# Convolution spans 12 to 15 of group 1 one a tile in tiles 2 to 5, with tile 0 reordered, span 31 moved to ScalarE and GpSimd, and the last sums in a free buffer

## The chip, the core and the metric

The kernel runs on one core of a Trainium2 chip. The metric is the device time of one execution in microseconds (us). Engines are named as the profile names them: PE (TensorE), DVE (VectorE), ACT (ScalarE), POOL (GpSimd), and SP, whose queue starts nearly all transfers.

## The reference

`x` is (128, 32, 512): 128 samples n, 32 channels c, 512 positions. Every (sample, channel) pair is one token of 512 values.

```python
y   = conv1d(x, weight, groups=4, kernel 9, padding 4) + cond @ c_weight.T + bias   # a shift per (n, c)
yq  = fake_quant(y,  per token)                  # scale = max|y| / 127, round, clip
h   = silu(yq @ wq_gate.T) * (yq @ wq_up.T)      # 512 -> 1376, weights fake-quantized per row
out = x + fake_quant(h, per token) @ wq_down.T   # 1376 -> 512
```

`fake_quant` rounds to whole steps of a scale that is the largest absolute value over 127, so a token can't be quantized before all of it is known.

## The kernel before

The 32 channels are 32 **tiles** of 128 tokens. Each tile goes through the same steps:

- PE multiplies the tile's quantized tokens by the gate and by the up weights, each in three **pieces** of 512, 512 and 352 columns (4 matmuls a piece, line 1043). Gate pieces go to PSUM banks 0 and 1, up pieces to 2 and 3, in turn, so a piece waits until the piece two before it in the same kind has been read out.
- DVE scales a gate piece (`scale_gate`, line 793), ACT takes SiLU (line 628), POOL multiplies by the weights' scales (`scale_silu`, line 517), and DVE multiplies by the up piece (`multiply_up`, line 803). Its last piece done, DVE takes the tile's largest value (`token_scales`, line 809), and ACT rounds (`round_h`, line 633) and converts (`convert_h`, line 641). SP's queue transposes the result.
- PE multiplies tile i - 4 by the down weights (`down`, 11 matmuls, line 1063), DVE scales it (line 821), POOL adds the residual (line 525), SP stores it.

The input of the tiles is made beside this. The convolution is done in four **groups** of 8 channels, and each group in eight **spans** of 64 positions, numbered 0 to 31: spans 8 to 15 are group 1, 24 to 31 group 3. A span is 5 float32 matmuls on PE (`conv_span`, line 927). Its result leaves PSUM in one of two ways: DVE adds the shift while it copies (`add_shift`, line 723), or, for the spans of the list `BY_ACT`, ACT copies (line 566) and POOL adds the shift later (`shift_span`, line 492). DVE folds two spans into running maxima (`fold_y`, line 735). After a group's last fold it makes the scale and the inverse, ACT rounds the group's channels (`round_y`, line 573), POOL converts them (line 482) and SP transposes them. Group 1 is needed from tile 8 on, group 3 from tile 24 on.

Tables set where this stands: `SPANS_AT` (the tile whose `for` body holds a span's matmuls and its reading), `SHIFTS_AT` (POOL's shifts), `FOLDS_AT` and `EARLY_FOLDS_AT` (DVE's folds), `CHANNELS_AT` (rounding and conversion). Every engine runs its own instructions strictly in the written order. In one tile PE's order is gate piece 0, gate 1, up 0, `down` of tile i - 4, the spans, gate 2, up 1, up 2; in tile 4 alone `down(0)` stands between up 1 and up 2. DVE's order in tile i is `scale_gate` 0, `multiply_up(i - 1, 2)`, `scale_gate` 1, `token_scales(i - 1)`, `multiply_up` 0, the down scaling, `scale_gate` 2, `add_shift`, `multiply_up` 1, the folds, and in tiles 0 to 2 the maxima of a quarter of the down weights (`weights_down`, line 711).

The first tiles also finish the weights: the last gate and up rows (`round_w(10)`, `turn_gate_up(10)`, `copy_gate_up(10)`), the rows of scales (`turn_xq`, `copy_xq`), and the down weights (`weights_down` on DVE, `round_down` on ACT line 578, `convert_down` on POOL line 473), one quarter a tile.

Of the kernel before, what the change touches and what calls it, by code (L numbers as in the profile page):

```python
# [27 lines left out]
def adaln_ffn(nc, x, x_windows, cond_ctx_bias, taps_cut, w_gate_up, w_down, out):  # L28
# [39 lines left out]
    with ExitStack() as ctx:  # L68
# [98 lines left out]

        BY_ACT = [2, 3, 4, 5] + list(range(SPANS, 2 * SPANS + 2))
        BY_DVE = [q for q in range(SLOTS) if q not in BY_ACT]
# [90 lines left out]

        SPANS_AT = {0: [9, 10], 1: [11], 2: [12, 13], 3: [14, 15]}
        SPANS_AT.update({5 + i: [16 + i] for i in range(SPANS)})
        SPANS_AT.update({17 + i: [24 + 2 * i, 25 + 2 * i] for i in range(SPANS // 2)})
# [13 lines left out]

        SHIFTS_AT = {1: [8, 9], 2: [10, 11], 3: [12, 13], 4: [14, 15], 5: [16], 6: [17]}
        EARLY_FOLDS_AT = {6: [15]}
        FOLDS_AT = {3: [9], 4: [11], 5: [13]}  # L280
        FOLDS_AT.update({i: [q for q in at if q % 2] for i, at in SPANS_AT.items() if at[0] >= 2 * SPANS + 2 and at[-1] % 2})
        FOLDS_AT[7] = [2 * SPANS + 1]

        def down_bank_of(i):
# [14 lines left out]
        def _(sp):  # L299
# [56 lines left out]
            def store(i):  # L356
                sp.wait_ge(out_ready, i + 1)
                sp.dma_start(out[:, i, :], xo_of(i))\
                    .then_inc(stored[i % XO_BUFS] if i < TILES - LATE else late_stored, 16)

            def store_last(half):
                cols = slice(HALF * half, HALF * (half + 1))
                sp.wait_ge(out_ready, TILES + half)
                sp.dma_start(out[:, TILES - 1, cols], xo_of(TILES - 1)[:, cols]).then_inc(late_stored, 16)
# [79 lines left out]
        def _(pool):  # L444
# [82 lines left out]
            for i in range(TILES):  # L527
                scale_silu(i, 0)
                if i == 0:
                    round_w(JT - 1)  # L530
                if i >= LAG + 1:
                    add_residual(i - LAG - 1)
                scale_silu(i, 1)
                if i == 0:

                    pool.wait_ge(w_turned, JT)
                    for b in range(HQ_BUFS):
                        pool.memset(hq[b][:, INTER:JT * P], 0.0).then_inc(pad_zero, 1)
                for o in down_at(i - 1):
                    convert_down(o)  # L540
                for n in EARLY_CHANNELS_AT.get(i, []):
                    convert_y(n)
                scale_silu(i, 2)
                for n in CHANNELS_AT.get(i, []):
                    convert_y(n)
                for q in SHIFTS_AT.get(i, []):
                    shift_span(q)
# [4 lines left out]
        def _(act):  # L552
# [92 lines left out]
            copy_xq(4)  # L645
            copy_span(8)
            silu(0, 1)
            copy_gate_up(8)
            copy_gate_up(9)
            copy_gate_up(10)  # L650
            copy_xq(5)
            copy_xq(6)
            for i in range(TILES):
# [3 lines left out]
                if i == DOWN_ROW_AT + 1:  # L657
                    copy_down_row()
                for o in down_at(i - 1):
                    round_down(o)  # L660
# [19 lines left out]
        def _(dve):  # L680
# [151 lines left out]
            for i in range(TILES):  # L832
# [12 lines left out]
                else:  # L845
                    for o in down_at(-1):
                        weights_down(o)
                folds(EARLY_FOLDS_AT.get(i, []))
                multiply_up(i, 0)
                if i == 0:  # L850
                    multiply_up(i, 1)
                    for o in down_at(0):
                        weights_down(o)
                if LAG < i < TILES - 1:
# [29 lines left out]
            def finish_last_but_one():  # L884
                i = TILES - 2
                dve.wait_ge(late_residuals_in, 16)

                dve.wait_ge(out_ready, i)
                dve.wait_ge(down_scaled, i + 1)
                dve.tensor_tensor(xo_of(i), xo_of(i), down_out[:, i % 2, :], ALU.add).then_inc(out_ready, 1)  # L890

            finish_last_but_one()

            def finish_last(half):
                i = TILES - 1
                cols = slice(HALF * half, HALF * (half + 1))
                part = down_out[:, i % 2, cols]
                if half == 0:

                    dve.wait_ge(out_ready, i - 1)  # L900
                dve.wait_ge(last_down_done, half + 1)
                dve.scalar_tensor_tensor(part, gate_bank[half][:, 0:HALF], h_scale[:, i:i + 1],
                                         wd_scale_row[:, cols], ALU.mult, ALU.mult).then_inc(last_down_scaled, 1)
                if half == 0:

                    dve.wait_ge(out_ready, i)
                dve.wait_ge(last_down_scaled, half + 1)
                dve.tensor_tensor(xo_of(i)[:, cols], xo_of(i)[:, cols], part, ALU.add).then_inc(out_ready, 1)

# [4 lines left out]
        def _(pe):  # L914
# [153 lines left out]
            for i in range(TILES):  # L1068
# [10 lines left out]
                if i == 0:  # L1079
# [5 lines left out]
                    turn_xq(5)  # L1085
                    turn_xq(6)
                if LAG < i < TILES - 1:
# [80 lines left out]
```

## Time and profile before

| | |
|---|---|
| median of 3 runs | 294.94 us (294.86 to 295.38) |
| the profiled execution | 295.01 us, of which its span is 293.4 us |
| granted TensorE clock | 1.00 |
| PE busy | 282.5 us, 96% of the span |
| DVE, ACT, POOL busy | 251.5, 194.1, 200.8 us |

The span runs from the first to the last instruction; 1.6 us of the execution lie around it. "Busy" of PE includes the pipelined ends of matmuls, so short waits between matmuls don't show as idle time on the page and are read from the chain of waits or from the weight loads.

### The profile page before, as it was taken

The numbers are of one execution on the slowest core, as the hardware profiler recorded it, in microseconds if no ns is written. First come the engines' busy times: TensorE is split into PE (matmuls) and PEld (weight loads), VectorE is DVE, ScalarE is ACT, GpSimd is POOL, SyncE is SP. The second block draws the span as 40 slices with busy tenths as digits, with TensorE's granted clock in tenths as the row PEclk, the third lists the DMA queues.
The fourth block names the chain that finished last, engine by engine and source line by source line (L and its number), as shares of the span: only waits on it lengthen the run. The fifth ranks groups of instructions, "written<-read, shape, count | busy, mean of one in ns | idle before, by whom it ended". The sixth has DMA issues, their size and how long they took to land.

```text
span 293.4 us, 4778 instructions
## 1 busy us (share of the span) xinstructions
PE 282.5 (96%) x1621; PEld 164.4 (56%) x1621; DVE 251.5 (86%) x406; ACT 194.1 (66%) x231; POOL 200.8 (68%) x212
## 2 busy tenths in 40 slices
PE   7998889999999999999999999999999999999994
PEld 7887656654555555555444566655444444444443
DVE  3879789999999997988988878898988889888885
ACT  2259889997777666654778845354788866666640
POOL 1595959998777667653788846552778887666623
PEclk9999999999999999999999999999999999999999
DMA  7999943479967867755389997526355683433345
GB/s 264 413 408 358 412 112 59 106 168 292 208 154 167 189 153 172 204 150 146 102 214 304 221 270 199 156 59 93 104 156 156 159 194 96 87 86 90 101 98 196
DMA packets 83847, 53.36 MB, mean 182 GB/s; under 512 B 69904, under 2 KB 70672, under 8 KB 83696
## 3 DMA queue, kind: packets, MB, share of 16 engines
q1 hardware_dynamic: 83536, 52.89, 67.3%
q10 hardware_dynamic: 288, 0.18, 0.3%
q8 instruction: 13, 0.21, 0.3%
q14 instruction: 10, 0.08, 0.1%
HBM read 27.75 MB, written 8.39 MB: 123 GB/s over the span
## 4 chain that ended last, share of the span: by engine, by line
PE 76%; DVE 11%; DMA 4%; POOL 3%; issue 2%; SPq 2%; ACT 1%; POOLq 1%; DVEq 0%
PE bank L1043 45%; PE bank L1063 21%; PE bank L927 9%; DMA slab<-x_windows 4%; DVE h_max L809 2%; DVE h_mem L803 2%; DVE gu_max L694 2%; DVE y_part L735 1%; SPq L308 1%; SPq L316 1%; POOL h_mem L465 1%; DVE sg_mem L793 1%; DVE y_mem L723 1%; POOL sg_mem L517 1%; POOLq L68 1%
## 5 line engine op out<-in xcount | busy, mean ns | idle before, releaser
L1043 PE MATMUL bank<-wgu_t,xq_mem 128*128 128x512 bf16 (+1 forms) x768 | 155.9, 357 | 1.5 <-DVE h_mem L803 1.0
L517 POOL TENSOR_TENSOR sg_mem<-sg_mem,gu_scale_row 128x512 f32<-128x512 f32 (+1 forms) x96 | 111.3, 1162 | 65.5 <-ACT sg_mem L628 65.5
L1043 PEld LDWEIGHTS bank<-wgu_t,xq_mem 128*128 128x128 bf16 x768 | 73.8, 98 | 73.6 <-DVE h_mem L803 8.4
L628 ACT ACTIVATE sg_mem<-sg_mem,x_scale 128x512 f32<-128x512 f32 (+1 forms) x96 | 63.6, 674 | 44.1 <-DVE sg_mem L793 43.7
L1063 PE MATMUL bank<-wd_t,hq_mem 128*128 128x512 bf16 (+1 forms) x341 | 78.6, 379 | 0.0
L803 DVE SCALAR_TENSOR_TENSOR h_mem<-bank,x_scale,sg_mem 128x512 f32<-128x512 f32 (+1 forms) x96 | 66.4, 692 | 11.8 <-POOL sg_mem L517 10.7
L793 DVE TENSOR_TENSOR sg_mem<-bank,gu_scale_row 128x512 f32<-128x512 f32 (+1 forms) x96 | 60.2, 628 | 14.3 <-PE bank L1043 14.1
L633 ACT ACTIVATE h_mem<-h_mem,h_inv 128x1376 f32<-128x1376 f32 (+1 forms) x32 | 45.3, 1415 | 28.7 <-DVE h_inv L687 28.6
L1063 PEld LDWEIGHTS bank<-wd_t,hq_mem 128*128 128x128 bf16 (+1 forms) x341 | 33.3, 98 | 40.4 <-DMA hq_mem<-hq_mem 0.5
L809 DVE TENSOR_REDUCE h_max<-h_mem 128x1 f32<-128x1376 f32 x32 | 50.5, 1577 | 0.0
L927 PE MATMUL bank<-toeplitz_cut,slab 128*128 128x160 f32 (+1 forms) x320 | 44.8, 291 | 2.4 <-DMA slab<-x_windows 1.8
L927 PEld LDWEIGHTS bank<-toeplitz_cut,slab 128*128 128x128 f32 x320 | 43.6, 191 | 5.6 <-DMA slab<-x_windows 2.6
L641 ACT ACTIVATE hq_mem<-h_mem 128x1376 bf16<-128x1376 f32 (+1 forms) x32 | 41.9, 1309 | 0.1
L525 POOL TENSOR_TENSOR xo_mem<-xo_mem,hq_mem 128x512 f32<-128x512 f32 x24 | 30.5, 1270 | 0.0
L821 DVE SCALAR_TENSOR_TENSOR hq_mem<-bank,h_scale,wd_scale_row 128x512 f32<-128x512 f32 x31 | 23.0, 743 | 1.3 <-POOL slab L525 1.3
L573 ACT ACTIVATE y_mem<-y_mem,x_inv 128x512 f32<-128x512 f32 x24 | 16.0, 707 | 0.3 <-DVE x_inv L687 0.3
L735 DVE TENSOR_REDUCE y_part<-y_mem 128x8 f32<-128x1024 f32 x12 | 14.6, 1215 | 1.7 <-POOL y_mem L492 1.6
L465 POOL TENSOR_SCALAR hq_mem<-hq_mem,gu_inv 128x512 f32<-128x512 f32 (+1 forms) x14 | 9.4, 692 | 6.5 <-DVE gu_inv L707 6.2
L482 POOL TENSOR_SCALAR yq_mem<-y_mem 128x512 bf16<-128x512 f32 x22 | 13.3, 620 | 0.2 <-ACT y_mem L573 0.2
L585 ACT ACTIVATE wgu_t<-bank 128x1024 bf16<-128x1024 int16 (+1 forms) x11 | 10.6, 1004 | 3.7 <-PE bank L943 3.6
L694 DVE TENSOR_REDUCE gu_max<-hq_mem 128x2 f32<-128x1024 f32 (+1 forms) x7 | 8.5, 1211 | 5.2 <-DMA hq_mem<-w_gate_up 5.2
L723 DVE TENSOR_TENSOR y_mem<-bank,shift 128x512 f32<-128x512 f32 x18 | 11.9, 681 | 0.7 <-PE bank L927 0.7
(63 smaller groups left out, 136.4 us busy)
## 6 DMA issues: line engine op xcount, KB each, us to landing
slab<-x_windows SPq DMA_DIRECT2D x32, 320.0 KB, 5.0
xo_mem<-x SPq DMA_DIRECT2D x24, 256.0 KB, 3.0
out<-xo_mem SPq DMA_DIRECT2D x24, 256.0 KB, 2.2
hq_mem<-w_gate_up SPq DMA_DIRECT2D x6, 512.0 KB, 6.7
slab<-w_down SPq DMA_DIRECT2D x3, 688.0 KB, 12.5
h_mem<-w_gate_up SPq DMA_DIRECT2D x4, 512.0 KB, 14.1
slab<-x SPq DMA_DIRECT2D x1, 2048.0 KB, 9.1
out<-slab SPq DMA_DIRECT2D x7, 256.0 KB, 2.0
```

What stands on the lines that cost most here:

```text
L517: pool.tensor_tensor(s, s, gu_scale_row[:, 1, at:at + n], ALU.mult).then_inc(silu_scaled, 1)
L525: pool.tensor_tensor(xo_of(i), xo_of(i), down_out[:, i % 2, :], ALU.add).then_inc(out_ready, 1)
L628: act.activation(s, s, ACT.Silu, scale=x_scale[:, i:i + 1]).then_inc(silu_done, 1)
L633: act.activation(hi, hi, ACT.Copy, bias=MAGIC, scale=h_inv[:, i:i + 1]).then_inc(h_rounded, 1)
L641: act.activation(hq[i % HQ_BUFS][:, first:INTER], h[i % H_BUFS][:, first:], ACT.Copy, bias=-MAGIC)\
L793: dve.tensor_tensor(sg[i % SG_BUFS][:, at:at + n], gate_bank[(NP * i + p) % 2][:, 0:n], gu_scale_row[:, 0, at:at + n], ALU.mult).then_inc( ...
L803: dve.scalar_tensor_tensor(h[i % H_BUFS][:, at:at + n], up_bank[(NP * i + p) % 2][:, 0:n], x_scale[:, i:i + 1], sg[i % SG_BUFS][:, at:at + ...
L809: dve.tensor_reduce(h_max[:, one], h[i % H_BUFS], AX_X, ALU.max, apply_absolute_value=True)\
L821: dve.scalar_tensor_tensor(down_out[:, i % 2, :], down_bank_of(i)[:, :], h_scale[:, i:i + 1], wd_scale_row[:, :], ALU.mult, ALU.mult).then ...
L927: last = pe.matmul(out_span[:, :, lo:hi], span_windows(g, i)[:, k, :], toeplitz_cut[:, g, :, tap:tap + hi - lo], start=(k == 0), stop=(k = ...
L1043: last = pe.matmul(bank[n % 2][:, 0:cols], xq_t[:, g, k, P * c:P * (c + 1)], wgu_t[:, m, k, at:at + cols], start=(k == 0), stop=(k == KT - 1))
L1063: last = pe.matmul(down_bank_of(i)[:, :], hq_t[i % HQT_BUFS][0:r, j, :], wd_t[0:r, j, :], start=(j == 0), stop=(j == JT - 1))
```

## The change

Four things are changed in the order of instructions; no matmul, copy or transfer is added or left out, but one read-out is done by other engines.

1. **Spans 12 to 15.** Before, tile 2 held spans 12 and 13, tile 3 held 14 and 15. Now tiles 2, 3, 4 and 5 hold one each (tile 5 also holds span 16). POOL's shifts 8 to 15 move along, some to the tile after.
2. **Tile 0.** ACT copies span 9 and the gate and up rows earlier and rounds the first quarter of the down weights ahead of `copy_xq(6)`. POOL rounds the last gate and up rows before its first `scale_silu` and shifts span 8. DVE takes the second quarter's maxima before the first two `multiply_up`. PE multiplies gate piece 2 before `turn_xq(6)`.
3. **Span 31.** ACT copies it and POOL adds the shift in tile 20, and DVE's last fold of group 3, with the group's scales, goes from tile 20 to tile 21.
4. **The last sums.** DVE's sums of tiles 30 and 31 count on semaphores of their own and no longer wait for POOL's sums, and tile 31's product goes to a free part of `sg_mem`.

```diff
-        BY_ACT = [2, 3, 4, 5] + list(range(SPANS, 2 * SPANS + 2))
+        BY_ACT = [2, 3, 4, 5] + list(range(SPANS, 2 * SPANS + 2)) + [SLOTS - 1]
...
-        SPANS_AT = {0: [9, 10], 1: [11], 2: [12, 13], 3: [14, 15]}
-        SPANS_AT.update({5 + i: [16 + i] for i in range(SPANS)})
+        SPANS_AT = {0: [10], 1: [11], 2: [12], 3: [13], 4: [14], 5: [15, 16]}
+        SPANS_AT.update({5 + i: [16 + i] for i in range(1, SPANS)})
...
-        SHIFTS_AT = {1: [8, 9], 2: [10, 11], 3: [12, 13], 4: [14, 15], 5: [16], 6: [17]}
+        SHIFTS_AT = {1: [9], 2: [10], 3: [11, 12], 4: [13], 5: [14, 15], 6: [16, 17], 20: [31]}
...
+        FOLDS_AT.pop(20)
+        FOLDS_AT[21] = [SLOTS - 1]
...
 # GpSimd
             scale_w(JT - 1, 1)
+            round_w(JT - 1)
...
                 scale_silu(i, 0)
-                if i == 0:
-                    round_w(JT - 1)
...
+                    shift_span(8)
...
 # ScalarE
             copy_span(8)
+            copy_gate_up(8)
             silu(0, 1)
-            copy_gate_up(8)
             copy_gate_up(9)
+            copy_span(9)
             copy_gate_up(10)
             copy_xq(5)
+            for o in down_at(-1):
+                round_down(o)
             copy_xq(6)
...
 # VectorE
+                if i == 0:
+                    for o in down_at(0):
+                        weights_down(o)
                 multiply_up(i, 0)
                 if i == 0:
                     multiply_up(i, 1)
-                    for o in down_at(0):
-                        weights_down(o)
...
-                dve.wait_ge(out_ready, i)
                 dve.wait_ge(down_scaled, i + 1)
-                dve.tensor_tensor(xo_of(i), xo_of(i), down_out[:, i % 2, :], ALU.add).then_inc(out_ready, 1)
+                dve.tensor_tensor(xo_of(i), xo_of(i), down_out[:, i % 2, :], ALU.add).then_inc(last_but_one_ready, 1)
...
-                part = down_out[:, i % 2, cols]
+                part = sg[(i - 1) % SG_BUFS][:, cols]
...
 # TensorE
-                    turn_xq(6)
...
                 gate_or_up(i, 0, 2)
-                if i:
+                if i == 0:
+                    turn_xq(6)
+                else:
                     gate_or_up(i, 1, 1)
```

**PE, tile 2**, from up piece 0 of tile 2 to up piece 2. `wgu_t` rows are gate (banks 0, 1) and up (banks 2, 3) pieces, `toeplitz_cut` rows are spans (three rows each). Before:

```order
L1043 MATMUL bank2<-wgu_t,xq_mem 128x512 x4
L927 MATMUL bank6<-toeplitz_cut,slab1 128x8x14
L927 MATMUL bank6<-toeplitz_cut,slab1 128x8x20 x3
L927 MATMUL bank6<-toeplitz_cut,slab1 128x8x14
L927 MATMUL bank7<-toeplitz_cut,slab1 128x8x14
L927 MATMUL bank7<-toeplitz_cut,slab1 128x8x20 x3
L927 MATMUL bank7<-toeplitz_cut,slab1 128x8x14
L1043 MATMUL bank0<-wgu_t,xq_mem 128x352 x4
L1043 MATMUL bank3<-wgu_t,xq_mem 128x512 x4
L1043 MATMUL bank2<-wgu_t,xq_mem 128x352 x4
```

and in the changed kernel:

```order
L1047 MATMUL bank2<-wgu_t,xq_mem 128x512 x4
L931 MATMUL bank6<-toeplitz_cut,slab1 128x8x14
L931 MATMUL bank6<-toeplitz_cut,slab1 128x8x20 x3
L931 MATMUL bank6<-toeplitz_cut,slab1 128x8x14
L1047 MATMUL bank0<-wgu_t,xq_mem 128x352 x4
L1047 MATMUL bank3<-wgu_t,xq_mem 128x512 x4
L1047 MATMUL bank2<-wgu_t,xq_mem 128x352 x4
```

The second span (bank 7) has left tile 2; it stands in tile 3, and tile 3's two spans have become one each in tiles 4 and 5.

**DVE, tiles 20 and 21**: the end of group 3, from `scale_gate` 2 of tile 20. `y_part` is the last fold, `y_max`, `x_scale` and `x_inv` the group's scales. Before:

```order
L793 TENSOR_TENSOR sg_mem<-bank0,gu_scale_row 128x352
L723 TENSOR_TENSOR y_mem<-bank6,shift 128x8x64
L723 TENSOR_TENSOR y_mem<-bank7,shift 128x8x64
L803 SCALAR_TENSOR_TENSOR h_mem<-bank3,x_scale,sg_mem 128x512
L735 TENSOR_REDUCE y_part<-y_mem 128x8
L740 TENSOR_REDUCE y_max<-y_part 128x8
L683 TENSOR_SCALAR x_scale<-y_max 128x8
L687 RECIPROCAL x_inv<-x_scale 128x8
L793 TENSOR_TENSOR sg_mem<-bank1,gu_scale_row 128x512
```

and in the changed kernel the same nine instructions' places in tile 20, and then the fold in tile 21:

```order
L803 TENSOR_TENSOR sg_mem<-bank0,gu_scale_row 128x352
L733 TENSOR_TENSOR y_mem<-bank6,shift 128x8x64
L813 SCALAR_TENSOR_TENSOR h_mem<-bank3,x_scale,sg_mem 128x512
L803 TENSOR_TENSOR sg_mem<-bank1,gu_scale_row 128x512
...
L813 SCALAR_TENSOR_TENSOR h_mem<-bank2,x_scale,sg_mem 128x512
L745 TENSOR_REDUCE y_part<-y_mem 128x8
L750 TENSOR_REDUCE y_max<-y_part 128x8
L693 TENSOR_SCALAR x_scale<-y_max 128x8
L697 RECIPROCAL x_inv<-x_scale 128x8
L803 TENSOR_TENSOR sg_mem<-bank0,gu_scale_row 128x512
```

One `add_shift` is gone from DVE, and four instructions stand one tile later.

**ACT, tile 0**, from the SiLU of piece 0 to that of piece 2. `wgu_t` rows are `copy_gate_up` 8, 9 and 10, `xq_mem` rows the copies of spans 8 and 9, `slab0` is `round_down(0)`. Before:

```order
L566 ACTIVATE xq_mem<-bank6 128x8x64
L628 ACTIVATE sg_mem<-sg_mem,x_scale 128x512
L585 ACTIVATE wgu_t<-bank4 128x8x128
L585 ACTIVATE wgu_t<-bank5 128x8x128
L585 ACTIVATE wgu_t<-bank4 128x8x96
L595 ACTIVATE gu_scale_row<-bank5 128x352
L595 ACTIVATE gu_scale_row<-bank4 128x352
L578 ACTIVATE slab0<-slab0,d_inv 128x1376
L628 ACTIVATE sg_mem<-sg_mem,x_scale 128x352
```

and in the changed kernel:

```order
L573 ACTIVATE xq_mem<-bank6 128x8x64
L592 ACTIVATE wgu_t<-bank4 128x8x128
L635 ACTIVATE sg_mem<-sg_mem,x_scale 128x512
L592 ACTIVATE wgu_t<-bank5 128x8x128
L573 ACTIVATE xq_mem<-bank7 128x8x64
L592 ACTIVATE wgu_t<-bank4 128x8x96
L602 ACTIVATE gu_scale_row<-bank5 128x352
L585 ACTIVATE slab0<-slab0,d_inv 128x1376
L602 ACTIVATE gu_scale_row<-bank4 128x352
L635 ACTIVATE sg_mem<-sg_mem,x_scale 128x352
```

`round_down(0)` and the last row of scales have changed places, and span 9's copy has come forward from behind the SiLU of piece 2.

## Rows read from the trace of the kernel before

**Rows 1.** The page: each engine's busy us, share of the span, instructions.

```profile
PE 282.5 (96%) x1621; PEld 164.4 (56%) x1621; DVE 251.5 (86%) x406; ACT 194.1 (66%) x231; POOL 200.8 (68%) x212
```

**Rows 2.** Busy time by stage: stretch, length, each engine's busy us, granted clock.

```profile
29.70:45.50 15.80, 13.59 (x95) 8.52 (x93) 12.49 (x21) 13.65 (x21) 12.45 (x17) 1.00 0.79 246
45.50:69.70 24.20, 24.16 (x138) 14.70 (x139) 23.23 (x38) 23.50 (x30) 23.42 (x24) 1.00 0.55 131
69.70:137.00 67.30, 67.30 (x366) 38.53 (x365) 60.94 (x100) 43.73 (x51) 46.31 (x45) 1.00 0.76 178
```

**Rows 3.** The chain of waits, tiles 2 to 5: start us, length us, what.

```profile
51.38 1.46 PE bank L1043 x8
...
52.87 3.36 PE bank L1043 x16
...
65.42 2.38 PE bank L1063 x11
67.79 3.19 PE bank L1043 x16
...
73.36 1.25 PE bank L927 x10
```

**Rows 4.** DVE's timeline, tiles 0 to 4: start, busy us, instruction, idle time before it.

```profile
37.41 1.58 DVE L711 TENSOR_REDUCE d_max<-slab 128x1 f32<-128x1376 f32 x1
...
41.66 0.58 DVE L803 SCALAR_TENSOR_TENSOR h_mem<-bank,x_scale,sg_mem 128x352 f32<-128x352 f32 x1 [1.25 <-POOL sg_mem L517]
...
44.70 0.75 DVE L803 SCALAR_TENSOR_TENSOR h_mem<-bank,x_scale,sg_mem 128x512 f32<-128x512 f32 x1
...
52.06 0.75 DVE L803 SCALAR_TENSOR_TENSOR h_mem<-bank,x_scale,sg_mem 128x512 f32<-128x512 f32 x1
...
59.35 0.75 DVE L803 SCALAR_TENSOR_TENSOR h_mem<-bank,x_scale,sg_mem 128x512 f32<-128x512 f32 x1
...
66.52 0.75 DVE L803 SCALAR_TENSOR_TENSOR h_mem<-bank,x_scale,sg_mem 128x512 f32<-128x512 f32 x1 [0.52 <-POOL sg_mem L517]
```

**Rows 5.** ACT's timeline, tile 0, and tiles 21 and 22.

```profile
36.02 0.81 ACT L585 ACTIVATE wgu_t<-bank 128x768 bf16<-128x768 int16 x1 [0.66 <-PE bank L943]
...
37.80 1.43 ACT L578 ACTIVATE slab<-slab,d_inv 128x1376 f32<-128x1376 f32 x1
39.85 0.59 ACT L628 ACTIVATE sg_mem<-sg_mem,x_scale 128x352 f32<-128x352 f32 x1 [0.62 <-DVE sg_mem L793]
...
209.88 1.32 ACT L573 ACTIVATE y_mem<-y_mem,x_inv 128x512 f32<-128x512 f32 x2
...
212.35 1.32 ACT L628 ACTIVATE sg_mem<-sg_mem,x_scale 128x512 f32<-128x512 f32 x2
```

**Rows 6.** POOL's timeline, tile 0.

```profile
34.06 1.35 POOL L465 TENSOR_SCALAR hq_mem<-hq_mem,gu_inv 96x512 f32<-96x512 f32 x2
...
40.63 0.93 POOL L517 TENSOR_TENSOR sg_mem<-sg_mem,gu_scale_row 128x352 f32<-128x352 f32 x1
```

**Rows 7.** PE's timeline: tile 21, and the two halves of `down_last`.

```profile
206.02 1.62 PE L1043 MATMUL bank<-wgu_t,xq_mem 128*128 128x352 bf16 x8
208.32 3.36 PE L1043 MATMUL bank<-wgu_t,xq_mem 128*128 128x352 bf16 x16 [0.68 <-DVE h_mem L803]
...
287.14 2.58 PE L1112 MATMUL bank<-wd_t,hq_mem 128*128 128x256 bf16 x22
```

**Rows 8.** DVE's timeline: tiles 20 to 22, and the last sums.

```profile
202.15 1.21 DVE L735 TENSOR_REDUCE y_part<-y_mem 128x8 f32<-128x1024 f32 x1
...
203.95 0.65 DVE L793 TENSOR_TENSOR sg_mem<-bank,gu_scale_row 128x512 f32<-128x512 f32 x1
...
214.54 0.75 DVE L803 SCALAR_TENSOR_TENSOR h_mem<-bank,x_scale,sg_mem 128x512 f32<-128x512 f32 x1 [0.36 <-POOL sg_mem L517]
...
288.58 0.69 DVE L890 TENSOR_TENSOR slab<-slab,hq_mem 128x512 f32<-128x512 f32 x1 [0.53 <-POOL slab L525]
...
290.11 0.48 DVE L902 SCALAR_TENSOR_TENSOR hq_mem<-bank,h_scale,wd_scale_row 128x256 f32<-128x256 f32 x1
```

More of the change, by code:

```diff
@@ L225, in adaln_ffn @@
         last_hq_ready = sem("last_hq_ready")
+        last_but_one_ready = sem("last_but_one_ready")
+        last_ready = sem("last_ready")
         h_rounded = sem("h_rounded")
@@ L356, in store @@
             def store(i):
-                sp.wait_ge(out_ready, i + 1)
+                if i < TILES - 2:
+                    sp.wait_ge(out_ready, i + 1)
+                else:
+                    sp.wait_ge(last_but_one_ready, 1)
                 sp.dma_start(out[:, i, :], xo_of(i))\
@@ L362, in store_last @@
                 cols = slice(HALF * half, HALF * (half + 1))
-                sp.wait_ge(out_ready, TILES + half)
+                sp.wait_ge(last_ready, half + 1)
                 sp.dma_start(out[:, TILES - 1, cols], xo_of(TILES - 1)[:, cols]).then_inc(late_stored, 16)
@@ L658, in _ @@
                     copy_down_row()
-                for o in down_at(i - 1):
+                for o in down_at(i - 1) if i else []:
                     round_down(o)
@@ L896, in finish_last @@
                 cols = slice(HALF * half, HALF * (half + 1))
-                part = down_out[:, i % 2, cols]
-                if half == 0:
-                    dve.wait_ge(out_ready, i - 1)
+                part = sg[(i - 1) % SG_BUFS][:, cols]
                 dve.wait_ge(last_down_done, half + 1)
@@ L903, in finish_last @@
                                          wd_scale_row[:, cols], ALU.mult, ALU.mult).then_inc(last_down_scaled, 1)
-                if half == 0:
-                    dve.wait_ge(out_ready, i)
                 dve.wait_ge(last_down_scaled, half + 1)
-                dve.tensor_tensor(xo_of(i)[:, cols], xo_of(i)[:, cols], part, ALU.add).then_inc(out_ready, 1)
+                dve.tensor_tensor(xo_of(i)[:, cols], xo_of(i)[:, cols], part, ALU.add).then_inc(last_ready, 1)
             for half in range(2):
@@ L1092, in _ @@
                 gate_or_up(i, 0, 2)
-                if i:
+                if i == 0:
+                    turn_xq(6)
+                else:
                     gate_or_up(i, 1, 1)
```

## The prediction, written before the result was known

> **What bounds the kernel now.** I read the page first: PE is busy for 282.5 us, 96% of the span [rows 1]. That points at PE, but a mean over stages doesn't say what a moved instruction costs, so the stages come next [rows 2]. From 69.7 to 137 us PE is busy for all 67.30 us and DVE for 60.94: there PE alone sets the pace, and a span more or less is paid in full. From 45.5 to 69.7 us (tiles 1 to 4) it is different: PE 24.16, ACT 23.50, POOL 23.42 and DVE 23.23 of 24.20 us. Who leads there must be read from order and waits. From 29.7 to 45.5 us (tile 0) PE is busy for 13.59 of 15.80 us and DVE for 12.49, so both wait.
>
> The chain of waits puts tiles 1 to 4 down to PE [rows 3], yet DVE runs just as tightly [rows 4]. Up piece 2 of a tile may start only when DVE has done `multiply_up` 0 of it. In tile 2 DVE starts that at 52.06 and takes 0.75, so it is done at 52.81; PE comes to the piece at 51.38 + 1.46 = 52.84 and starts it at 52.87. The two engines arrive together. DVE's steps from tile to tile are 52.06 - 44.70 = 7.36 and 59.35 - 52.06 = 7.29 us, with no idle time in between. So with its two spans in each of tiles 2 and 3, PE has exactly as much work as DVE's step is long. This is the fact on which the forecast stands.
>
> **Part 1, tile 0: DVE comes out about 1.25 us earlier.** DVE waited 1.25 us and began `multiply_up(0, 2)` at 41.66 [rows 4], for POOL's `scale_silu(0, 2)` at 40.63 [rows 6]. POOL was held by ACT's `round_down(0)`, which began at 37.80, and behind it ACT took the SiLU at 39.85 [rows 5]. ACT in turn waited 0.66 us and began `copy_gate_up(10)` at 36.02, for rows that POOL rounded only from 34.06 to 35.41, behind a `scale_silu`. Now that rounding goes first and is ready before PE gets to turn the rows at about 34.9. I put the copy at about 35.35, 0.67 earlier. Between that copy and `round_down(0)` lay 37.80 - 36.02 = 1.78 us with two rows of scales; the second, `copy_xq(6)`, now comes behind, which takes an estimated 0.7 with the wait before it. So `round_down(0)` begins at 36.4 and `copy_xq(6)` is done at 38.2. Gate piece 2 is scaled by 38.75, its SiLU (0.59) is done at 39.4, `scale_silu` (0.93) at 40.4, and `multiply_up(0, 2)` starts at 40.4 where it started at 41.66: **1.25 us earlier**. The second quarter's maxima (1.58, before at 37.41) stand in the time in which DVE waits for POOL anyway, and span 8's shift stands where POOL was idle: both at nothing. If that cover is gone, each is late by what it takes: 1.6, and for the shift at most 1.35 (POOL's 0.93 for 352 columns [rows 6], scaled to 512).
>
> From there DVE keeps its order with no idle time, so `multiply_up` 0 of tiles 1, 2 and 3 starts at 43.45, 50.8 and 58.1. Its steps stay 7.36 and 7.29 us, since nothing in DVE's tiles 1 to 3 has changed.
>
> **Part 2, the spans: +2.5 us.** One span takes PE 1.25 us [rows 3]. Two spans leave tiles 2 and 3. PE then has 3.19 + 1.46 for the pieces [rows 3] and 1.25 for a span, 5.9 us of work in a DVE step of 7.3 and waits about 1.4 us before up piece 2 in each of tiles 2 and 3. The spans stand again in tiles 4 and 5. Tile 4 is where `down` begins (2.38 a tile) and where DVE no longer takes weight maxima (before, it even had 0.52 us idle at 66.52 [rows 4]). So there PE sets the pace and pays 1.25 us for each. Checked along the path: up piece 2 of tile 3 now starts at 58.1 + 0.75 + 0.05 = 58.9, before at 59.35 + 0.75 + 0.05 = 60.15. From there to the end of `down(0)` PE needed 67.80 - 60.15 = 7.65 us, now 7.65 + 1.25 = 8.9. That ends at 67.8, the time of before, and span 15 is still owed. Parts 1 and 2 make -1.25 + 2.5 = **+1.25 us**, and from tile 5 on PE has no gap that takes it back.
>
> Group 1's later spans cost nothing more: the copies and shifts of tile 5 fall where ACT and POOL are busy for only 43.73 and 46.31 of 67.30 us [rows 2], and DVE folds span 15 only behind `token_scales(5)`, by my count some 2 us after the shift. That room hides them.
>
> **Part 3, span 31: +0.4 us.** Before, DVE's two `add_shift`, the fold and the group's scales (202.15 to 203.95, that is 1.80 us [rows 8]) pushed `multiply_up(21, 0)` back, and PE waited 0.68 us at 208.32 [rows 7]. Its next 16 matmuls took 3.36 us against 3.19 without a wait [rows 3], so 0.85 in all. That wait goes: DVE has an `add_shift` and 1.80 us less in tile 20. But the fold now starts behind `multiply_up(21, 1)`, which is done at about 206.2 + 1.46 + 0.75 = 208.4, so the inverses are there at 208.4 + 1.80 + 0.1 = 210.3. ACT has `round_y` twice, then `convert_h(20)`, then the SiLU of tile 22 in its order; the first three took 212.35 - 209.88 = 2.47 us [rows 5], so this SiLU starts at 212.8. Before, 214.54 - 212.35 = 2.19 us lay from that SiLU to `multiply_up(22, 0)` [rows 5, 8], which now starts at 215.0 and ends at 215.7. PE comes to up piece 2 of tile 22 at 206.2 + 4.65 + 2.38 + 1.46 = 214.7. It waits about 1.1 us and restarts 0.17 slower, 1.25 in all where 0.85 was paid: +0.4.
>
> **Part 4, the last sums: -0.3 us.** DVE waited 0.53 us for POOL's sum and began tile 30's sum at 288.58; the last half began at 290.11 [rows 8]. Freed, DVE could be 0.5 us earlier, but PE's second half ends at 287.14 + 2.58 = 289.72 [rows 7], and with 0.1 to pass that on DVE starts the last half at 289.8: **-0.3**. Both ends: 0 if the sums can't run beside POOL's, -0.5 if the modelled end of PE is late.
>
> The sum is +1.25 + 0.4 - 0.3 = +1.35 on the profiled execution's 295.01, 296.4. The median of the runs shown is 0.07 lower, so I forecast **296.3 us**.
>
> **A page against this.** DVE's sum of tile 30 now starts while POOL's last residual sum runs, and no row of before has a DVE instruction with two operands in SBUF beside a working POOL. If they can't run together, DVE still starts at about 288.5 and the -0.3 is lost: 296.6. The Trainium skill says just this (SBUF — State Buffer, "Who interferes with whom"): a DVE instruction with two SBUF inputs contends with a GpSimd instruction that reads SBUF, and the later one is blocked for the whole of the other. No row here shows it.
>
> **The rivals.**
> - *The last sums gain nothing*: 296.6, chance 0.17.
> - *Faster: PE, not DVE, leads in tiles 2 and 3.* Then the spans cost the same wherever they stand, and tile 0's 1.25 us arrive whole: 294.94 - 1.25 + 0.4 - 0.3 = 293.8. For it speaks that the chain of waits names PE all through tiles 2 to 5 [rows 3]. Against it: `multiply_up` ends 0.06 us before PE's start in tile 2, and DVE has no idle time to give. It decides at DVE's step: the two steps would have to shrink by 1.25 us together before this breaks even. Chance 0.10.
> - *Group 3's new chain isn't late*: part 3 becomes -0.85, and the time 296.3 - 1.25 = 295.0. It needs the inverses 1.1 us earlier than I have them. Chance 0.13.
> - *Something hidden comes due in tiles 3 to 6*, where POOL now has two shifts a tile three times: one shift on the path, at 1.0 (between 0 and 1.35), gives 297.3. POOL's room from 69.7 on speaks against it, its 23.42 of 24.20 us before that for it [rows 2]. Chance 0.10.
>
> **How the numbers follow.** The forecast has 0.50. Its own range is 295.7 to 296.9: tile 0's gain within 0.3, part 3 within 0.4, part 4's ends. A measurement of this kernel tells about 0.2% (0.6 us) from no change, so "same" is 294.35 to 295.53. Slower: most of the forecast, the page's case and the last rival, 0.67. Same: the third rival and the forecast's low edge, 0.21. Faster: the second rival and a little for errors that add up, 0.12. The range, 294.8 to 297.0, leaves out the faster case and the far end of the last.
>
> **What would show it.** PE waits of 1.2 to 1.5 us before up piece 2 of tiles 2 and 3 that name DVE's `multiply_up`, where before there was 0.1; `multiply_up(0, 2)` at 40.4 and `down(0)` ending at about 67.8, as before, with span 15 behind it. In tile 22 a wait of about 1.1 us in place of tile 21's 0.68. DVE's last half starting at 289.8 relative to a `down_last` at 287.14. The prediction is wrong if DVE's step falls below 7.2 us, if `multiply_up(0, 2)` isn't earlier, or if PE shows waits in tiles 4 to 12.

## The result, and the profile after

The changed kernel takes **296.29 us** (median of 6 runs, 296.27 to 296.4) against 294.90 us (6 runs, 294.85 to 295.38): ratio 1.004, 95% interval 1.0028 to 1.0052, so it is slower by about 0.4%. The forecast was 296.3 us. The profiled execution took 296.40 us with a span of 294.8 us.

The page of the changed kernel, engine shares and the gate and up matmuls (columns: busy, mean ns | idle time before them, and who ended most of it):

```profile
PE 281.7 (96%) x1621; PEld 164.1 (56%) x1621; DVE 251.2 (85%) x405; ACT 194.4 (66%) x232; POOL 202.0 (69%) x213
...
L1047 PE MATMUL bank<-wgu_t,xq_mem 128*128 128x512 bf16 (+1 forms) x768 | 156.1, 357 | 5.2 <-DVE h_mem L813 4.4
```

PE's work is the same as in [rows 1] to 1 us. What grew is idle time ahead of gate and up matmuls that DVE's `multiply_up` (now line 813) ends: 4.4 us in four waits (0.93, 1.14, 1.17 and 1.13 us, all shown below), where the view of waits of the kernel before has 1.0 us in two. The windows say where (columns as in [rows 2]):

```profile
29.70:45.50 15.80, 14.20 (x102) 9.22 (x101) 13.62 (x23) 14.86 (x22) 14.98 (x19) 1.00 0.82 248
45.50:69.70 24.20, 21.89 (x124) 12.89 (x123) 22.95 (x37) 22.27 (x28) 21.32 (x22) 1.00 0.62 153
69.70:137.00 67.30, 67.30 (x371) 39.27 (x370) 59.00 (x95) 43.74 (x51) 46.08 (x44) 1.00 0.73 170
```

In tile 0 PE, DVE, ACT and POOL all get more done. In tiles 1 to 4 PE loses 2.3 us of busy time, and from 69.7 to 137 us it has no gap, as before. PE's and then DVE's timeline of the changed kernel, tiles 0 to 4:

```profile
44.39 3.36 PE L1047 MATMUL bank<-wgu_t,xq_mem 128*128 128x352 bf16 x16 [0.93 <-DVE h_mem L813]
...
48.83 1.62 PE L1047 MATMUL bank<-wgu_t,xq_mem 128*128 128x352 bf16 x8
51.59 3.36 PE L1047 MATMUL bank<-wgu_t,xq_mem 128*128 128x352 bf16 x16 [1.14 <-DVE h_mem L813]
54.79 1.41 PE L931 MATMUL bank<-toeplitz_cut,slab 128*128 128x112 f32 x10
...
58.83 0.77 PE L1047 MATMUL bank<-wgu_t,xq_mem 128*128 128x352 bf16 x4 [1.17 <-DVE h_mem L813]
...
65.17 2.54 PE L1067 MATMUL bank<-wd_t,hq_mem 128*128 128x512 bf16 x11
67.55 3.35 PE L1047 MATMUL bank<-wgu_t,xq_mem 128*128 128x352 bf16 x16
70.74 2.54 PE L1067 MATMUL bank<-wd_t,hq_mem 128*128 128x512 bf16 x11
```

```profile
40.60 0.58 DVE L813 SCALAR_TENSOR_TENSOR h_mem<-bank,x_scale,sg_mem 128x352 f32<-128x352 f32 x1 [0.87 <-POOL sg_mem L525]
...
43.58 0.75 DVE L813 SCALAR_TENSOR_TENSOR h_mem<-bank,x_scale,sg_mem 128x512 f32<-128x512 f32 x1
...
50.79 0.75 DVE L813 SCALAR_TENSOR_TENSOR h_mem<-bank,x_scale,sg_mem 128x512 f32<-128x512 f32 x1
...
58.02 0.75 DVE L813 SCALAR_TENSOR_TENSOR h_mem<-bank,x_scale,sg_mem 128x512 f32<-128x512 f32 x1
```

Beside [rows 4]: `multiply_up(0, 2)` comes 1.06 us earlier (41.66 to 40.60), and DVE's steps are 7.21 and 7.23 us. PE, with one span in each of tiles 2 and 3, waits 1.14 and 1.17 us there.

These printed waits are 0.16 us short of what PE loses. In the timeline the record of a run of matmuls overlaps the next run: the 16 matmuls at 67.55, which wait for nothing, have a record of 3.35 us, and the next start comes after 70.74 - 67.55 = 3.19. So losses of PE are best read from start to start. The eight matmuls at 48.83 take 1.46 us to the next start where nothing is waited for (in tile 4 they start at 63.71 and `down` at 65.17). So the next ones could have started at 50.29 and started at 51.59, **1.30 us** late. In tile 3 it is 1.33 in the same way. The 16 matmuls behind the wait are not slower: 54.79 - 51.59 = 3.20 us.

`down(0)` starts at 65.17, 0.08 us earlier than in the kernel before, with span 15 still owed. In PE's timeline of the kernel before:

```profile
65.25 2.54 PE L1063 MATMUL bank<-wd_t,hq_mem 128*128 128x512 bf16 x11
```

With span 15 paid in tile 5 the offset between the kernels is constant up to tile 21; the chain of waits of both shows the same eight matmuls 1.19 us apart, first before, then after:

```profile
132.52 1.47 PE bank L1043 x8
```

```profile
133.71 1.47 PE bank L1047 x8
```

Tiles 21 and 22 of the changed kernel, timelines of PE, then ACT, then DVE:

```profile
207.21 4.81 PE L1047 MATMUL bank<-wgu_t,xq_mem 128*128 128x352 bf16 x24
...
216.99 3.49 PE L1047 MATMUL bank<-wgu_t,xq_mem 128*128 128x352 bf16 x16 [1.13 <-DVE h_mem L813]
```

```profile
211.51 1.34 ACT L580 ACTIVATE y_mem<-y_mem,x_inv 128x512 f32<-128x512 f32 x2 [2.06 <-DVE x_inv L697]
212.75 1.33 ACT L648 ACTIVATE hq_mem<-h_mem 128x1376 bf16<-128x1376 f32 x1
213.99 1.32 ACT L635 ACTIVATE sg_mem<-sg_mem,x_scale 128x512 f32<-128x512 f32 x2
```

```profile
216.18 0.75 DVE L813 SCALAR_TENSOR_TENSOR h_mem<-bank,x_scale,sg_mem 128x512 f32<-128x512 f32 x1 [1.18 <-POOL sg_mem L525]
```

The wait of tile 21 is gone (24 matmuls in one piece), and one of 1.13 us has come in tile 22. ACT stood 2.06 us for group 3's inverses with a conversion and a SiLU queued behind. PE's first matmuls behind `down` in tile 21 are 1.19 us late (206.02 to 207.21); by tile 23 it is 1.63, and at `down_last` 1.71 (287.14 [rows 7] to 288.85).

The end, timelines of PE, POOL and DVE:

```profile
288.85 2.58 PE L1117 MATMUL bank<-wd_t,hq_mem 128*128 128x256 bf16 x22
```

```profile
286.41 3.72 POOL L533 TENSOR_TENSOR slab<-slab,hq_mem 128x512 f32<-128x512 f32 x3 [5.18 <-DVE hq_mem L831]
```

```profile
288.96 0.75 DVE L831 SCALAR_TENSOR_TENSOR hq_mem<-bank,h_scale,wd_scale_row 128x512 f32<-128x512 f32 x1 [0.50 <-POOL slab L533]
289.82 0.86 DVE L900 TENSOR_TENSOR slab<-slab,hq_mem 128x512 f32<-128x512 f32 x1
...
291.47 0.48 DVE L909 SCALAR_TENSOR_TENSOR sg_mem<-bank,h_scale,wd_scale_row 128x256 f32<-128x256 f32 x1
```

The last half starts 0.04 us behind PE's end (288.85 + 2.58 = 291.43), where it started 290.11 - 289.72 = 0.39 behind it [rows 7, 8]. Tile 30's sum began 0.31 us before POOL's last sum was done (286.41 + 3.72 = 290.13) and took 0.86 us instead of 0.69.

### The profile page after: what moved, and what is told of

It is laid out like the page before. It is cut to its first block, busy times and chain, and to the rows that moved or that the text cites. A ratio compares the mean times of both kernels' runs of the same rounds, so it can differ in the third digit from the quotient of the medians.

```text
span 294.8 us, 4778 instructions
## 1 busy us (share of the span) xinstructions
PE 281.7 (96%) x1621; PEld 164.1 (56%) x1621; DVE 251.2 (85%) x405; ACT 194.4 (66%) x232; POOL 202.0 (69%) x213
## 4 chain that ended last, share of the span: by engine, by line
PE 71%; DVE 11%; POOL 5%; DMA 4%; ACT 4%; issue 3%; SPq 1%; DVEq 0%; POOLq 0%
PE bank L1047 42%; PE bank L1067 20%; PE bank L931 8%; DMA slab<-x_windows 3%; DVE h_max L819 3%; DVE h_mem L813 2%; POOL sg_mem L525 2%; DVE sg_mem L803 1%; DVE y_part L745 1%; DMA hq_mem<-hq_mem 1%; DVE gu_max L704 1%; POOL y_mem L499 1%; ACT wgu_t L592 1%; SPq L320 1%; ACT sg_mem L635 1%
## 5 line engine op out<-in xcount | busy, mean ns | idle before, releaser
L733 DVE TENSOR_TENSOR y_mem<-bank,shift 128x512 f32<-128x512 f32 x17 | 11.2, 680 | 0.6 <-PE bank L931 0.6
```

## The experiments

The changed kernel's row is that of the result, beside its own before (294.90 us); it was not run again beside the experiments. The first four ran on one chip, beside a before of 294.99 us (10 runs). The next four ran on another chip, which scattered more (before 295.46 us, 17 runs, 294.83 to 296.35). Its profiled executions differ by up to 0.7 us in how late tile 0 begins. To compare traces I subtract that: the four matmuls behind `copy_gate_up(10)`, at 36.35 in the changed kernel, are the mark, and "by the trace" below means behind this mark. Experiments 9 and 10 had one run each, on a third chip (before 295.45 us, one run).

| experiment | us, median | ratio to before, 95% interval |
|---|---|---|
| changed kernel | 296.29 | 1.0040 (1.0028 to 1.0052) |
| 1 spans back | 293.72 | 0.9958 (0.9946 to 0.9971) |
| 2 spans only | 297.45 | 1.0082 (1.0069 to 1.0096) |
| 3 tile 0 only | 293.61 | 0.9952 (0.9938 to 0.9965) |
| 4 span 31 back | 295.90 | 1.0030 (1.0019 to 1.0042) |
| 5 last sums back | 296.91 | 1.0054 (1.0034 to 1.0074) |
| 6 conversion first | 295.35 | 0.9997 (0.9985 to 1.0010) |
| 7 spans back, conversion first | 292.92 | 0.9916 (0.9898 to 0.9933) |
| 8 as 7, spans earlier | 292.73 | 0.9908 (0.9890 to 0.9926) |

**1. Spans back.**

```diff
-        SPANS_AT = {0: [10], 1: [11], 2: [12], 3: [13], 4: [14], 5: [15, 16]}
-        SPANS_AT.update({5 + i: [16 + i] for i in range(1, SPANS)})
+        SPANS_AT = {0: [10], 1: [11], 2: [12, 13], 3: [14, 15]}
+        SPANS_AT.update({5 + i: [16 + i] for i in range(SPANS)})
-        SHIFTS_AT = {1: [9], 2: [10], 3: [11, 12], 4: [13], 5: [14, 15], 6: [16, 17], 20: [31]}
+        SHIFTS_AT = {1: [9], 2: [10, 11], 3: [12, 13], 4: [14, 15], 5: [16], 6: [17], 20: [31]}
```

> The changed kernel with one part undone: spans 12 to 15 stand two a tile in tiles 2 and 3 again, with their shifts; tile 0, span 31 and the last sums stay changed. My theory: in tiles 2 and 3 DVE sets the step, so the moved spans leave PE idle there (1.14 + 1.17 us before up piece 2 in the changed kernel) and are paid in tiles 4 and 5. Put back, PE's waits there fall to about 0.1, PE leads, and tile 0's 1.06 us arrive only as far as PE now sets the step: 296.3 less 1.9 to 2.4, so 293.9 to 294.4 us. Rival: PE leads in tiles 2 and 3 and a span costs the same wherever it stands; then this kernel takes what the changed one takes, 296.3 us, and the loss lies elsewhere (span 31).

Measured: 293.72 us, 2.57 less than the changed kernel and a little under what my theory gave. PE's timeline, tiles 1 to 3:

```profile
44.24 3.36 PE L1047 MATMUL bank<-wgu_t,xq_mem 128*128 128x352 bf16 x16 [0.93 <-DVE h_mem L813]
47.44 2.67 PE L931 MATMUL bank<-toeplitz_cut,slab 128*128 128x112 f32 x20
49.95 4.86 PE L1047 MATMUL bank<-wgu_t,xq_mem 128*128 128x352 bf16 x24
54.65 2.67 PE L931 MATMUL bank<-toeplitz_cut,slab 128*128 128x112 f32 x20
57.15 2.30 PE L1047 MATMUL bank<-wgu_t,xq_mem 128*128 128x352 bf16 x12
```

Both waits of over 1.1 us are gone, with all else as it was. The spans moved out of tiles 2 and 3 are the loss. From start to start PE lost 1.30 + 1.33 = 2.63 us there in the changed kernel. Here it still stands for 0.05 us in tile 2 (54.65 - 49.95 = 4.70 us, where 24 matmuls without a wait take 211.86 - 207.21 = 4.65 in the changed kernel) and for 0.07 in tile 3. That leaves 2.51 us, and the traces agree: `down(0)` starts 27.57 us behind the mark here and 28.82 in the changed kernel, which still owes a span of 1.25 us. The rival falls.

**2. Spans only.** The same four spans moved in the kernel before, nothing else.

```diff
-        SPANS_AT = {0: [9, 10], 1: [11], 2: [12, 13], 3: [14, 15]}
-        SPANS_AT.update({5 + i: [16 + i] for i in range(SPANS)})
+        SPANS_AT = {0: [9, 10], 1: [11], 2: [12], 3: [13], 4: [14], 5: [15, 16]}
+        SPANS_AT.update({5 + i: [16 + i] for i in range(1, SPANS)})
```

> The kernel before with the spans alone moved: 12 to 15 one a tile in tiles 2 to 5, their shifts along; nothing else changed. My theory: two spans at 1.25 us leave tiles in which DVE sets the step and are paid in tiles 4 and 5, +2.3 to +2.5 us: 297.2 to 297.4 us, with a wait of some 1.2 us before up piece 2 of tiles 2 and 3 that names DVE's multiply_up, whose start at 52.06 and 59.35 does not move. Rival: the spans cost the same in either place: 294.9 us, and no wait of that size.

Measured: 297.45 us, +2.46. PE's waits in tiles 2 and 3:

```profile
52.71 3.36 PE L1043 MATMUL bank<-wgu_t,xq_mem 128*128 128x352 bf16 x16 [1.28 <-DVE h_mem L803]
60.01 0.77 PE L1043 MATMUL bank<-wgu_t,xq_mem 128*128 128x352 bf16 x4 [1.23 <-DVE h_mem L803]
```

And the chain of waits, which in [rows 3] ran through PE alone in these tiles, now runs through DVE:

```profile
53.05 0.75 DVE h_mem L803
53.80 1.50 DVE d_max L711
...
57.38 1.50 DVE h_max L809
...
59.20 0.76 DVE h_mem L803
60.01 0.77 PE bank L1043 x4
```

The reader sees the hidden second bound appear: the same DVE instructions, at nearly the same distances (7.35 and 7.30 us from `multiply_up` 0 to the next tile's), that in the kernel before were level with PE.

**3. Tile 0 only.** The kernel before with the reordering of tile 0. Of its edits the two that stand on the path of part 1 (they were not run apart from the others):

```diff
+            round_w(JT - 1)
...
             for i in range(TILES):
                 scale_silu(i, 0)
-                if i == 0:
-                    round_w(JT - 1)
...
             copy_xq(5)
+            for o in down_at(-1):
+                round_down(o)
             copy_xq(6)
```

> The kernel before with tile 0's order alone changed (the rounding of the last row, the order of copies, the early rounding of down's rows, the maxima ahead of multiply_up, span 8's shift). My theory: multiply_up(0, 2) starts about 1.06 us earlier, as in the changed kernel. With two spans in tiles 2 and 3 PE was level with DVE there, so PE can follow by only a part of this before it leads itself: between 0 and -1.06, most likely -0.9 to -1.06 if PE's own idle time of tile 0 shrinks with it: 293.9 to 294.0 us. Rival: PE is already the bound from tile 1 on and the gain does not pass tile 2: 294.9 us.

Measured: 293.61 us, -1.38, more than I gave it, and the rival falls. In the traces PE starts up piece 2 of tile 1 1.11 us earlier (45.51 to 44.40) and `down(0)` 1.31 earlier (65.25 to 63.94). So 0.2 us more are won in tiles 2 and 3. DVE's own steps got shorter by that much, and PE, which followed DVE there, stood less for it: in the kernel before the 24 matmuls of tile 2 took 4.85 us from start to start, 0.20 more than without a wait, and here 4.70. In the kernel before DVE's `multiply_up(1, 1)` stood for POOL; the timelines of POOL and DVE there:

```profile
43.32 2.52 POOL L517 TENSOR_TENSOR sg_mem<-sg_mem,gu_scale_row 128x512 f32<-128x512 f32 x2 [0.59 <-ACT sg_mem L628]
```

```profile
45.37 0.52 DVE L793 TENSOR_TENSOR sg_mem<-bank,gu_scale_row 128x352 f32<-128x352 f32 x1
45.94 0.75 DVE L803 SCALAR_TENSOR_TENSOR h_mem<-bank,x_scale,sg_mem 128x512 f32<-128x512 f32 x1
```

POOL was done at 45.84 and DVE began at 45.94. In the changed kernel the same pair stands at 44.25 and 44.68, which is 0.14 closer, because POOL was done at 44.33. A gap this short is not printed as idle time by the view, and I had taken its absence for none. (The profiled execution of this experiment, 294.00 us, is the slowest of its five: PE's weight loads wait 0.51 us for a transpose at 75.49, behind the stretch read here.)

**4. Span 31 back.**

```diff
-        BY_ACT = [2, 3, 4, 5] + list(range(SPANS, 2 * SPANS + 2)) + [SLOTS - 1]
+        BY_ACT = [2, 3, 4, 5] + list(range(SPANS, 2 * SPANS + 2))
-        FOLDS_AT.pop(20)
-        FOLDS_AT[21] = [SLOTS - 1]
```

> The changed kernel with one part undone: span 31 goes back to DVE and its fold to tile 20. My theory (the offset between the two traces grew from 1.19 to 1.63 us across tiles 20 to 23): the wait of tile 22 goes, that of tile 21 (0.68 and a slower restart) comes back, 0.44 less: 295.85 us. Rival: without the wait of tile 22, PE is caught by another late piece of the group's scales and the time stays at 296.3 us.

Measured: 295.90 us, 0.39 less. PE waits in tile 21 again, and in tile 22 no more than in the kernel before (0.14 us from start to start there, and 0.15 before, which the view doesn't print):

```profile
209.44 3.36 PE L1045 MATMUL bank<-wgu_t,xq_mem 128*128 128x352 bf16 x16 [0.67 <-DVE h_mem L811]
```

**5. Last sums back.**

```diff
+                dve.wait_ge(out_ready, i)
                 dve.wait_ge(down_scaled, i + 1)
-                part = sg[(i - 1) % SG_BUFS][:, cols]
+                part = down_out[:, i % 2, cols]
```

> The changed kernel with one part undone: the last sums wait as before (tile 30's sum for POOL's last residual sum, the last halves for the sum before them). My theory: the last half starts 0.3 us later behind PE's last matmuls, as in the kernel before (290.11 against a down_last at 287.14): 296.6 us, and the wait of 0.5 us for POOL's sum is back. Rival: the sums had gained nothing, since DVE's sum beside POOL's got slower (0.86 against 0.69 us): 296.3 us.

Measured: 296.91 us on the scattered chip. Its interval overlaps that of the changed kernel, so the time does not decide. The trace does as far as one execution can: the last half starts at 291.79 against PE's end of 288.89 + 2.58 = 291.47, 0.32 behind it, where it is 0.04 in the changed kernel.

```profile
290.26 0.69 DVE L898 TENSOR_TENSOR slab<-slab,hq_mem 128x512 f32<-128x512 f32 x1 [0.35 <-POOL slab L530]
...
291.79 0.48 DVE L910 SCALAR_TENSOR_TENSOR hq_mem<-bank,h_scale,wd_scale_row 128x256 f32<-128x256 f32 x1
```

**6. Conversion first.**

```diff
+                if i == 21:
+                    convert_h(i - 1)
                 for n in CHANNELS_AT.get(i, []):
                     round_y(n)
...
-                if i:
+                if i and i != 21:
                     convert_h(i - 1)
```

> The changed kernel with one more edit: in tile 21 ACT's convert_h(20) stands ahead of the two round_y of group 3, not behind them. My theory: span 31's cost comes through ACT, where the conversion and the SiLU of tile 22 stand behind two round_y that wait 2.06 us for the inverses. What goes ahead is the conversion alone (0.65 us and its wait), so the SiLU comes 0.6 to 1.2 us earlier and PE's wait of 1.13 us in tile 22 falls to 0 to 0.5: 295.0 to 295.7 us. Rival: the wait in tile 22 comes from DVE's own fold and scales and not from ACT; then nothing changes, 296.3 us.

Measured: 295.35 us, ratio 0.9997, level with the kernel before; by the trace 1.2 us less than the changed kernel. ACT's timeline:

```profile
209.43 1.33 ACT L648 ACTIVATE hq_mem<-h_mem 128x1376 bf16<-128x1376 f32 x1
211.59 1.34 ACT L580 ACTIVATE y_mem<-y_mem,x_inv 128x512 f32<-128x512 f32 x2 [0.82 <-DVE x_inv L699]
212.83 1.32 ACT L635 ACTIVATE sg_mem<-sg_mem,x_scale 128x512 f32<-128x512 f32 x2
```

The conversion (1.24 us to the next start, not the 0.65 that I had written) fills the time in which ACT stood idle, the SiLU comes 1.24 us earlier behind the mark, and in tile 22 PE has no wait left that the view prints. From start to start its 24 matmuls there take 219.17 - 214.32 = 4.85 us, so 0.20 of the wait is left. The rival, that DVE's own fold is what is late, falls.

**7. Spans back and conversion first.** The edits of 1 and 6 together.

> The changed kernel with the spans two a tile again in tiles 2 and 3, and ACT's convert_h(20) ahead of the two round_y in tile 21. If the two parts add up: 296.3 less 1.9 to 2.4 for the spans and less 0.6 to 1.3 for the conversion: 292.6 to 293.8 us. Rival: the two waits take each other's place (one tile's earlier start is lost at the next late buffer) and the time is no less than with the spans put back alone, 294.1 us.

Measured: 292.92 us, ratio 0.9916: the two add up, and this is 2.5 us faster than the kernel before.

**8. Spans earlier.** Against the kernel of experiment 7:

```diff
-        SPANS_AT = {0: [10], 1: [11], 2: [12, 13], 3: [14, 15]}
+        SPANS_AT = {0: [10], 1: [11, 12], 2: [13, 14], 3: [15]}
```

> As the kernel with the spans back and the conversion first, and span 12 one tile earlier still: spans 11 and 12 in tile 1, 13 and 14 in tile 2, 15 in tile 3. My theory: PE waited 0.93 us in tile 1 for DVE in the changed kernel. A span there fills that wait (1.25 us of work for 0.93 of idle time), and tile 3 has room again: up to 0.9 us less, so 291.8 to 292.9 us. Rival: the span in tile 1 needs its channels earlier than ACT rounds them, or DVE's step from tile 1 to 4 is the bound whatever PE does: no less than with the spans back, 292.6 to 293.8 us.

Measured: 292.73 us, which can't be told from experiment 7; by the trace the two are within 0.1 us. My theory here was wrong, and the half of the rival that names DVE's step held. The wait of tile 1 goes, and one of 1.16 us comes in tile 3:

```profile
58.78 0.77 PE L1049 MATMUL bank<-wgu_t,xq_mem 128*128 128x352 bf16 x4 [1.16 <-DVE h_mem L815]
```

Up piece 2 of tile 3 starts when DVE gets there, whatever PE did before. A span won in tile 1 only moves the idle time, unless another span is there to put in tile 3. Span 16 can't be taken for it as the code stands, since its windows are loaded in tile 4 and its buffer is group 0's; that wasn't tried.

**9 and 10. A DVE instruction beside POOL's last sums.** The changed kernel with one more instruction, ahead of the third of the last four `scale_down`, its result unread; in 9 a sum of two SBUF tiles, in 10 a scaling of one:

```diff
+                    dve.tensor_tensor(s[:, 0:512], s[:, 0:512], s[:, 512:1024], ALU.add)
```

```diff
+                    dve.tensor_scalar(s[:, 0:512], s[:, 512:1024], 1.0, 0.0, ALU.mult, ALU.add)
```

> The changed kernel with one more instruction, whose result nothing reads: a DVE sum of two 128x512 SBUF tiles, placed where DVE waits 0.79 us for POOL's second-last residual sums (286.93 in the changed kernel's trace, while POOL works from 286.41 to 290.13 without a gap). Question: does a DVE instruction with two SBUF operands stand still beside a POOL sum. If it does, it starts at about 286.95 and lasts until the POOL sum under way ends at about 287.65 and some 0.55 more, so it shows 1.2 to 1.3 us in place of 0.69. If the two share the port at a small price, it shows 0.7 to 0.9 us. The time hardly moves by either, since DVE has 0.8 and 0.5 us of waits there: 296.3 to 296.9 us.

> The control to the kernel with the sum of two SBUF tiles: at the same place a DVE scaling of one 128x512 SBUF tile. Whatever holds up two operands, one operand of this kind should start at about 286.95 and take its usual time, which for 1024 columns was 0.75 us and so for 512 is 0.4 to 0.5 us. If it takes 1 us or more too, the hold-up isn't one of two operands.

Measured: 297.35 and 296.72 us, one run each. 9 is beyond what I expected: its last half starts at 292.45, 0.48 us behind PE's end (289.39 + 2.58), so the added time was not hidden. The sum of two tiles, DVE's timeline, and POOL's three residual sums (their shortest, median and longest in ns):

```profile
287.39 1.38 DVE L896 TENSOR_TENSOR sg_mem<-sg_mem 128x512 f32<-128x512 f32 x1
```

```profile
L533 POOL TENSOR_TENSOR slab<-slab,hq_mem x3: 1267/1270/1717, 287.0 to 289.9; 128x512 f32<-128x512 f32 x3
```

The scaling of one tile, the same two views:

```profile
287.02 1.12 DVE L896 TENSOR_SCALAR sg_mem<-sg_mem 128x512 f32<-128x512 f32 x1
```

```profile
L533 POOL TENSOR_TENSOR slab<-slab,hq_mem x3: 1269/1272/1448, 286.6 to 289.2; 128x512 f32<-128x512 f32 x3
```

In 9 POOL's first sum runs from 286.96 to about 288.23. DVE's sum lasts until 287.39 + 1.38 = 288.77, so 0.54 us beyond it: 0.69 more than it takes by itself [rows 8]. It stood still until POOL's instruction under way was done. POOL's next one, at 288.19, took 1.72 us, 0.45 longer, while DVE was at work. In 10 DVE ends at 288.14, 0.28 behind POOL's first sum (286.59 + 1.27 = 287.86). So the control was held up too, and my expectation of 0.4 to 0.5 us for it was wrong. The Trainium skill (SBUF — State Buffer, "Who interferes with whom") says both: the lock is exclusive for a whole instruction, and a `tensor_scalar` can take it as well, in a two-port mode. The hold-ups of both runs agree with it; which mode the scaling ran in, no run shows. Only one of POOL's three sums is long in each run, and it is the one behind the hand-over: DVE had to wait for one POOL instruction and not for the three.

## Why the prediction was right, point by point

**The fact it stood on: PE and DVE level in tiles 2 and 3.** Shown from both sides. Experiments 1 and 2 move the same four spans, in the changed kernel and in the kernel before, and the price is 2.57 and 2.46 us where the text had 2.5. The faster rival (PE leads, the spans cost the same wherever they stand, 293.8 us) has fallen by both. "Level" was not quite so: from start to start PE already stood for DVE in the kernel before, 0.20 us in tile 2 (56.06 - 51.21 = 4.85 against 4.65 us) and 0.13 in tile 3. So DVE led in both, by little, and tile 0's gain arrives whole in experiment 3, where the spans stay. PE's timeline of the kernel before:

```profile
51.21 5.01 PE L1043 MATMUL bank<-wgu_t,xq_mem 128*128 128x352 bf16 x24
56.06 2.67 PE L927 MATMUL bank<-toeplitz_cut,slab 128*128 128x112 f32 x20
```

**Part 1 (tile 0, -1.25).** The sum was right to 0.1 us and its terms were not. `round_down(0)` began at 36.44 and the SiLU was done at 39.42, where the text had 36.4 and 39.4. But behind it the text left out two hand-overs, to POOL (its `scale_silu` began at 39.56) and back to DVE (from 40.49 to 40.60), so `multiply_up(0, 2)` came 1.06 us earlier, not 1.25. In exchange "its steps stay 7.36 and 7.29" failed: they fell to 7.21 and 7.23, since POOL, earlier too, no longer held up `multiply_up` 1 of tiles 1 and 2 (by 0.14 and about 0.05). Together DVE is 59.35 - 58.02 = 1.33 us earlier in tile 3. That two terms missed by 0.2 us in opposite directions is luck.

**Part 2 (spans, +2.5).** Right by its steps. PE's work from one up piece 2 to the next is 5.90 us, as the text had it; with DVE's steps of 7.21 and 7.23 that leaves 1.31 and 1.33, and PE lost 1.30 and 1.33 from start to start, where some 1.4 was named. `down(0)` comes 0.08 us earlier, where no change was named, with span 15 owed. No wait is printed in tiles 4 to 12, as the text asked. Parts 1 and 2 gave +1.19 where +1.25 stood. The condition "wrong if DVE's step falls below 7.2 us" was nearly met, by 0.01 us in tile 1. At a step of 7.2 the spans still cost almost all of their price, so that bound was drawn too tight.

**Part 3 (span 31, +0.4).** Measured +0.44 by the trace and 0.39 by experiment 4. Experiment 6 shows the path that the text named, through ACT's queue and not through DVE's: with the conversion moved ahead of the rounding that waits, the same late inverses cost PE 0.20 us in tile 22, and 0.15 of that it stood there before, too (218.69 - 213.89 = 4.80 against 4.65). One reading in this part is wrong though its number holds: PE does not "restart 0.17 slower". 3.36 and 3.19 us are the same 16 matmuls, once counted from their own start and once from the end of the record before them, and the 0.17 us is part of the wait.

**Part 4 (last sums, -0.3).** The last half's start moved from 0.39 to 0.04 us behind PE's end, 0.35; against experiment 5 it is 0.28. The size was right, and the rival's mechanism is real (experiment 9), but its price wasn't: `scale_down(30)` starts only at 288.96, when PE's `down(30)` (288.86) and POOL's second sum (288.91) are done, so DVE comes to its own sum with only 0.31 us of POOL's last one left. That adds 0.17 us to its record: it ends 0.55 us behind POOL's sum, as the one of experiment 9 does (0.54), where a free one takes 0.69. Perhaps part of its start passes while it stands; no run shows that. The last half starts 0.04 us behind PE's end, so the 0.17 us can hardly have cost anything. That this holds in the median too stays open, since experiment 5's time does not tell the two apart.

The measured parts are 1.19 + 0.44 - 0.35 us, and 0.08 that no part had: PE reaches `down_last` 1.71 us late, not 1.63. Most of it falls on the last `down` matmuls, where PE now waits for a transposed tile (0.22 us in the timeline at 286.31). Together 1.36 us, the distance of the two last halves (290.11 to 291.47), against 296.40 - 295.01 = 1.39 between the two profiled executions.

## What to carry to other kernels

Before moving work out of a stage, ask which engine sets its step. Where two engines are level, the chain of waits names one of them, and taking work from that one buys nothing while the place it goes to pays in full; moving the work back, with the other engine made earlier, turned +0.4% into -0.4%. When a late result is waited for in an in-order queue, look at what stands behind the wait: putting the work that is ready ahead of it (one conversion, 1.2 us) was worth more here than making the result itself earlier (experiment 4, 0.4 us).

## What the runs showed of the hardware that I had not expected

A DVE scaling from SBUF to SBUF of one 128x512 tile stood still beside a POOL sum (1.12 us; by itself it was not run, but one of 1024 columns takes 0.75 at 284.60 in experiment 9), as a sum of two operands did (1.38 against 0.69 us). Both engines pay: POOL's next sum took 1.72 and 1.45 us against 1.27. A DVE instruction with one operand in PSUM was not held up beside the same POOL sums: `scale_down` took 0.75 us there (289.93 in experiment 9), as at 286.07 in the kernel before.

```profile
289.93 0.75 DVE L831 SCALAR_TENSOR_TENSOR hq_mem<-bank,h_scale,wd_scale_row 128x512 f32<-128x512 f32 x1 [0.50 <-POOL slab L533]
```
